# Eight buffers instead of four for the expert tiles' results and their addresses

## The chip, the cores and the metric

The kernel runs on 1 core of one Trainium2 chip. The metric is the device time of one execution in microseconds (us), the median of several runs. A profile of one further execution goes with it.

## The reference

Four stages work on x, 4 sequences of 512 tokens with 128 features. The second and the fourth are the same mixture of experts, with the same weights; the change lies in both.

```
x = x + attention(layernorm(x))
x = x + ffn(layernorm(x))        # list 0 of the kernel
x = x + scan_block(layernorm(x))
x = x + ffn(layernorm(x))        # list 1 of the kernel

# ffn, for each of the 2048 tokens:
scores = sigmoid(xf @ Wg.T + bg + bias)                  # 8 experts
top_scores, top_idx = top_k(scores, 2)
h  = gelu(einsum('td,ehd->teh', xf, W1) + b1)            # 128 -> 512
eo = einsum('teh,edh->ted', h, W2) + b2                  # 512 -> 128
combined = einsum('ted,te->td', eo, weights)             # the 2 chosen experts
shared   = gelu(xf @ Ws1.T + bs1) @ Ws2.T + bs2
```

## The kernel before

Each engine has its own stream of instructions, in an order written out by hand, and semaphores join them. In the ffn every token row is first scattered to `rows_dram` at a place sorted by expert, twice (once for each chosen expert). Then the sorted rows are worked off as a list of NT = 39 tiles of 128 rows, each of one expert. The results are scattered back to `y_dram` in token order, read again in four pieces and added to x with their weights (`combine`). The program has two such lists of 39 tiles, 78 tiles in all.

Every engine goes through a list in a loop over k. LAG is 3, so that in one turn of the loop different tiles are at different steps:

- SyncE (SP) loads the rows of tile s into `xg`, one of 7 buffers (L491). Load n waits until GpSimd has taken the addresses of tile n-7 (`goes_to_ready`) and TensorE has turned that tile.
- TensorE (PE): `turn(k)` transposes tile k (L1182, 2 matmuls), `up(k-1)` adds the bias (L1189, 4) and multiplies by W1 (L1194, 12), `down(k-3)` multiplies by W2 (L1205, 12).
- ScalarE (ACT): the gelu (L831) into `hid_t` and its high half (L836).
- VectorE (DVE), in this order in a turn of the loop: `turned(k)` copies the transposed tile to `xgT` (L1636), `low(k-2)` makes the low half of the hidden values (L1642), `results(k-3)` copies the result from PSUM to `y_t` (L1650).
- GpSimd (POOL): `address(k)` makes the rows of `y_dram` to which tile k goes, first `result_row` (L652), then `goes_to` (L654), and `store(k-3)` issues the indirect DMA from `y_t` to `y_dram` (L661), which reads its addresses from `goes_to`.

`y_t`, `result_row` and `goes_to` have YT buffers each. Two waits guard them, in `address` on GpSimd and in `results` on VectorE. Both ask that the scatter of tile n-YT has landed:

```
if n >= YT:
    pool.wait_ge(y_stored[n % YT], 16 * (n // YT))     # address(s), ahead of L652
...
if n >= YT:
    dve.wait_ge(y_stored[n % YT], 16 * (n // YT))      # results(s), ahead of L1650
```

The scatter of tile k-4 is issued in turn k-1 of GpSimd's loop, straight ahead of `address(k)`. After a list SyncE waits for every `y_stored` semaphore before it reads `y_dram` back (L497). `xgT`, `hid_t` and `y_t` are parts of one SBUF tensor, `arena`; the profile shows them, `yg` and the shared expert's `hid` under that name. The profile's `probs` is `hid16_t` in the lists, `qk_sb` is `xg`, and `heads_arena` holds other stages' tiles.

Of the kernel before, what the change touches and what calls it, by code (L numbers as in the profile page):

```python
# [10 lines left out]
F16 = mybir.dt.float16  # L11
# [3 lines left out]
P = 128  # L15
D = 128
# [9 lines left out]
F = 512  # L26
# [73 lines left out]
SPARE = P * NT + 2  # L100
RESULTS = SPARE + 2 * B * L
TILES_OF = B * L // P
XG, GT, HT, YT = 7, 3, 3, 4
LAG = 3
S_AT = TILES_OF
ROW_AT = S_AT + NT
# [71 lines left out]
def hybrid_block_kernel(nc, x_in, wqkv_in, wo_in, bo_in, w1_in, b1_in, w2_in, b2_in, wg_in, gate_rows_in,  # L178
# [3 lines left out]
    with ExitStack() as ctx:  # L182
        def sb(name, shape, dt=F32):
            return ctx.enter_context(nc.sbuf_tensor(name, shape, dt))
# [102 lines left out]
        arena = sb("arena", [P, 2 * X * F])  # L287
# [15 lines left out]
        def part(t, at, shape, dt=F32):  # L303
            size = int(np.prod(shape)) * (1 if dt == F32 else 2) // (1 if dt == F32 else 4)
            names = " ".join("abcd"[:len(shape)])
            sizes = dict(zip("abcd", shape))
            flat = t[:, at:at + size]
            return (flat if dt == F32 else flat.bitcast(dt)).rearrange(f"p ({names}) -> p {names}", **sizes)
# [10 lines left out]
        hid = part(arena, 0, [C, L])  # L319
        hid16 = part(arena, 2048, [2, C, L], F16)  # L320
        yg = part(arena, 4096, [2, TT, 2, D])
        xgT = part(arena, 6656, [GT, 2, P], F16)
        hid_t = part(arena, 7040, [HT, F])
        y_t = part(arena, 8576, [YT, D])
        xcv = part(probs_words, 0, [2, 2, L])
        hid16_t = part(probs_words, 2048, [HT, 2, F], F16)
        bias_tmp = heads_arena[:, 2048:3072]
# [1532 lines left out]
```

## Time and profile before

| | |
|---|---|
| median of 3 runs | 892.85 us (888.28 to 895.38) |
| profiled execution, its own time | 894.25 us |
| span of that execution | 892.4 us |
| TensorE / VectorE / ScalarE / GpSimd busy | 67% / 52% / 39% / 39% of the span |
| list 0, first to last scatter of results issued | 392.34 to 546.44 us |
| list 1, first to last scatter of results issued | 720.02 to 871.86 us |

Busy time is the share of the whole span. The profile's chain of waits goes back from the last instruction through what released each step, so its lines are time that the end of the program stood on. The times inside the profile belong to the one profiled execution, which took 894.25 us, 1.4 us more than the median.

### The profile page before, as it was taken

To read this page: it belongs to the slowest core of one execution; us is meant where nothing else is said; L and a number is where in the kernel's file an instruction comes from. 1 tells how busy PE (TensorE), PEld (TensorE's weight loads), DVE (VectorE), ACT (ScalarE), POOL (GpSimd) and SP (SyncE) were. 2 spreads that over 40 slices of the span, in tenths; PEclk is the share of its full clock that TensorE was granted. 3 is DMA by queue.
4 is the path that set the end of the run, shared out by engine and by line. 5 is a ranking of instruction groups with operands and counts; after the bars stand their busy time and mean duration, and the time that the engine had idled before them with its cause. 6 is when DMAs were issued, how large, how long until landed. Compare 5 with 4: busy or idle time off the path is not lost. (4 is left out here: it accounts for less than half of the span.)

```text
span 892.4 us, 16950 instructions
## 1 busy us (share of the span) xinstructions
PE 594.1 (67%) x5836; PEld 402.2 (45%) x5836; DVE 466.1 (52%) x1241; ACT 344.4 (39%) x462; POOL 349.9 (39%) x447
## 2 busy tenths in 40 slices
PE   2588888888885635578776750567676588676730
PEld 1454445444443413466655640234354376555520
DVE  5877776776772555533222221678867543222214
ACT  1355456556652424335332320225254354332310
POOL 4152080190001575534544453114335445444550
PEclk9699999999997757789877785667687799877875
DMA  8995000000000000111110102100000111111104
GB/s 297 328 334 161 2 1 1 1 2 1 1 2 27 24 7 28 38 45 38 31 31 25 37 19 77 35 0 25 7 19 24 35 46 32 31 30 31 35 18 150
DMA packets 45146, 46.37 MB, mean 52 GB/s; under 512 B 5369, under 2 KB 42386, under 8 KB 44810
## 3 DMA queue, kind: packets, MB, share of 16 engines
q1 hardware_dynamic: 40522, 35.91, 13.5%
q0 software_dynamic: 4544, 9.38, 3.1%
q8 instruction: 52, 0.85, 0.4%
q14 instruction: 28, 0.23, 0.1%
HBM read 16.75 MB, written 28.52 MB: 51 GB/s over the span
## 5 line engine op out<-in xcount | busy, mean ns | idle before, releaser
L1650 DVE COPY arena<-ps 128x128 f32<-128x128 f32 x78 | 22.7, 292 | 211.3 <-DMA y_dram<-arena,goes_to 177.4
L831 ACT ACTIVATE arena<-ps,up_back 128x512 f32<-128x512 f32 x78 | 53.6, 687 | 194.5 <-PE ps L1194 194.5
L1194 PE MATMUL ps<-arena,w 128*128 128x128 f16 x936 | 96.6, 246 | 45.3 <-DVE arena L1636 45.0
L1384 DVE TENSOR_REDUCE row_maxima<-ps 128x2 f32<-128x256 f32 (+3 forms) x128 | 99.0, 817 | 42.8 <-PE ps L958 42.5
L710 ACT ACTIVATE probs<-ps 128x768 f32<-128x768 f32 (+1 forms) x96 | 82.5, 884 | 81.2 <-PE ps L983 81.2
L512 POOL TENSOR_TENSOR rstd<-var_eps,minus_half 128x4 f32<-128x4 f32 x16 | 17.0, 1060 | 222.6 <-DVE var_eps L1321 222.6
L1205 PE MATMUL ps<-w,probs 128*128 x936 | 95.2, 248 | 10.8 <-DVE probs L1642 10.7
L1194 PEld LDWEIGHTS ps<-arena,w 128*128 x936 | 72.2, 106 | 65.9 <-issue 55.5
L661 POOL DMA_INDIRECT y_dram<-arena,goes_to x78 | 85.0, 1090 | 34.5 <-POOL goes_to L654 20.9
L643 POOL DMA_INDIRECT rows_dram<-probs,idx x64 | 69.0, 1078 | 52.8 <-DVE idx L1582 33.0
L1205 PEld LDWEIGHTS ps<-w,probs 128*128 128x128 f16 x936 | 77.0, 111 | 21.9 <-issue 12.3
L652 POOL TENSOR_SCALAR result_row<-qk_sb,list_end 128x1 f32<-128x1 f32 x78 | 29.4, 377 | 132.0 <-DMA y_dram<-arena,goes_to 120.9
L1003 PE MATMUL ps<-probs,v_tok 128*16 128x256 f32 (+3 forms) x512 | 74.7, 434 | 2.5 <-ACT probs L710 2.5
L1642 DVE SCALAR_TENSOR_TENSOR probs<-arena,hid_scale,probs 128x512 f16<-128x512 f32 x78 | 58.2, 746 | 4.5 <-ACT probs L836 4.5
L836 ACT ACTIVATE probs<-arena,hid_scale 128x512 f16<-128x512 f32 x78 | 56.3, 721 | 2.6
L1189 PE MATMUL ps<-which,bias_rows 128*128 128x128 bf16 x312 | 37.4, 254 | 20.4 <-issue 20.0
L654 POOL TENSOR_SCALAR goes_to<-result_row,grids 128x1 int32<-128x1 f32 x78 | 46.7, 599 | 7.3
L1003 PEld LDWEIGHTS ps<-probs,v_tok 128*16 128x16 f32 x512 | 24.2, 96 | 47.7 <-issue 35.4
L953 PE MATMUL ps<-heads_arena 48*128 48x128 bf16 (+3 forms) x256 | 37.6, 308 | 11.6 <-DVE row_maxima L1384 6.4
L978 PE MATMUL ps<-q2T,heads_arena 50*128 50x512 bf16 (+3 forms) x256 | 38.5, 310 | 9.0 <-ACT probs L710 7.2
L1189 PEld LDWEIGHTS ps<-which,bias_rows 128*128 128x128 bf16 x312 | 22.1, 112 | 32.2 <-issue 31.4
L1159 PE MATMUL ps<-w,arena 128*128 128x128 f16 x384 | 26.2, 230 | 13.3 <-DVE arena L1616 8.9
(234 smaller groups left out, 1111.7 us busy)
## 6 DMA issues: line engine op xcount, KB each, us to landing
rows_dram<-grids SPq DMA_DIRECT2D x2, 8840.0 KB, 44.1
qk_sb<-rows_dram SPq DMA_DIRECT2D x78, 65.0 KB, 1.8
arena<-in_w SPq DMA_DIRECT2D x2, 2304.0 KB
arena<-y_dram SPq DMA_DIRECT2D x8, 512.0 KB, 4.0
y_dram<-arena,goes_to POOLq DMA_INDIRECT x78, 2.4
x_all<-in_x SPq DMA_DIRECT2D x4, 256.0 KB, 8.1
rows_dram<-probs,idx POOLq DMA_INDIRECT x64
out_x<-x_all SPq DMA_DIRECT2D x4, 256.0 KB, 3.7
```

The costliest lines, as they stand in the source:

```text
L643: nc.gpsimd.indirect_dma_start(rows_dram[r].ap(), bass.IndirectOffsetOnAxis(ap=idx[:, r, b, t, k:k + 1], axis=0), xrow_words[:, b % 2, t, ...
L654: nc.gpsimd.tensor_scalar(goes_to[:, n % YT:n % YT + 1], result_row[:, n % YT:n % YT + 1], grids[:, SPARE_AT + s:SPARE_AT + s + 1], None, ...
L661: nc.gpsimd.indirect_dma_start(y_dram.ap(), bass.IndirectOffsetOnAxis(ap=goes_to[:, n % YT:n % YT + 1], axis=0), y_t[:, n % YT, :], None). ...
L710: nc.scalar.activation(probs[:, n % 2, :, PROB_AT[u]:PROB_AT[u] + size], ps[:, of:of + 2, 0:size], ACT.Exp).then_inc(slot_free[slot_of(("T ...
L831: nc.scalar.activation(hid_t[:, n % HT, :], ps[:, of, :], ACT.Gelu, scale=up_back[:]).then_inc(bank_free[of], 1)
L836: nc.scalar.activation(hid16_t[:, n % HT, 0, :], hid_t[:, n % HT, :], ACT.Identity, scale=hid_scale[:]).then_inc(high_t_ready, 1)
L1003: mm = pe.matmul(ps[quadrant:quadrant + VW, PV_BANK, j * P:L], v_tok[:, a % 2, j, 2 * p + h, :], probs[:, n % 2, h, at:at + size], start=( ...
L1189: pe.matmul(ps[:, to, c * P:(c + 1) * P], bias_rows[:, c * P:(c + 1) * P], which[:, s:s + 1].broadcast_to([P, P]), start=(c == 0), stop=Fa ...
L1194: mm = pe.matmul(ps[:, to, c * P:(c + 1) * P], w1[:, w, bass.ds(expert[s], 1), c * P:(c + 1) * P].rearrange("p o f -> p (o f)"), xgT[:, (r ...
L1205: mm = pe.matmul(ps[:, to, 0:D], hid16_t[:, n % HT, v, c * P:(c + 1) * P], w2[:, w, bass.ds(expert[s], 1), c, :].rearrange("p o d -> p (o ...
L1384: ins = nc.vector.tensor_reduce(row_maxima[:, t, 2 * p:2 * p + 2], ps[:, of:of + 2, o:o + keys], AX.X, ALU.max)
L1642: nc.vector.scalar_tensor_tensor(hid16_t[:, n % HT, 1, :], hid_t[:, n % HT, :], hid_scale[:], hid16_t[:, n % HT, 0, :], ALU.mult, ALU.subt ...
```

## The change

YT goes from 4 to 8. `y_t`, `result_row` and `goes_to` get 8 buffers, there are 8 `y_stored` semaphores, and the two waits above ask for tile n-8. To make room in the arena, `xgT`, `hid_t` and `y_t` start 512 words earlier, directly behind `yg` (which ends at word 6144); `y_t` ends at word 9088 as before. Neither an instruction nor the order on an engine changes; the waits do. SyncE waits for 8 semaphores in place of 4 after each list.

```diff
-XG, GT, HT, YT = 7, 3, 3, 4
+XG, GT, HT, YT = 7, 3, 3, 8
...
-        xgT = part(arena, 6656, [GT, 2, P], F16)
-        hid_t = part(arena, 7040, [HT, F])
-        y_t = part(arena, 8576, [YT, D])
+        xgT = part(arena, 6144, [GT, 2, P], F16)
+        hid_t = part(arena, 6528, [HT, F])
+        y_t = part(arena, 8064, [YT, D])
```

GpSimd's stream in list 0 before, from the first scatter on (L661, store(0)): each following L652 waits for the scatter that stands just ahead of it.

```order
138 L661 DMA y_dram<-arena,goes_to 9090x128 [waits bank_free1,goes_to_ready]
139 L652 TENSOR_SCALAR result_row<-qk_sb,list_end 128x1 [waits y_stored0,xg_loaded4]
140 L654 TENSOR_SCALAR goes_to<-result_row,grids 128x1 [waits pool_step]
141 L661 DMA y_dram<-arena,goes_to 9090x128 [waits bank_free4,goes_to_ready]
142 L652 TENSOR_SCALAR result_row<-qk_sb,list_end 128x1 [waits y_stored1,xg_loaded5]
```

The same place with the change: the four L652 of tiles 4 to 7 wait for their rows alone.

```order
138 L661 DMA y_dram<-arena,goes_to 9090x128 [waits bank_free1,goes_to_ready]
139 L652 TENSOR_SCALAR result_row<-qk_sb,list_end 128x1 [waits xg_loaded4]
140 L654 TENSOR_SCALAR goes_to<-result_row,grids 128x1 [waits pool_step]
141 L661 DMA y_dram<-arena,goes_to 9090x128 [waits bank_free4,goes_to_ready]
142 L652 TENSOR_SCALAR result_row<-qk_sb,list_end 128x1 [waits xg_loaded5]
```

The first `y_stored0` on GpSimd now stands at tile 8, whose wait is for the scatter of tile 0, issued five turns of the loop before. On VectorE the same is seen at L1650, here in the difference of the two streams for tiles 4 and 5:

```order
-L1650 COPY arena<-ps 128x128 [waits y_stored0,bank_full5]
 L1636 COPY arena<-ps 128x256 [waits bank_full1,bank_full6]
 L1642 SCALAR_TENSOR_TENSOR probs<-arena,hid_scale,probs 128x512 [waits high_t_ready]
-L1650 COPY arena<-ps 128x128 [waits y_stored1,bank_full0]
+L1650 COPY arena<-ps 128x128 [waits bank_full0]
```

Only the semaphore of the scatter has left the row; the bank that TensorE fills (`bank_full`) stays.

## Rows read from the trace of the kernel before

**Rows 1.** The page's chain that ended last, by line
```profile
DMA y_dram<-arena,goes_to 10%; POOL goes_to L654 2%; POOL result_row L652 1%; DMA arena<-y_dram 1%; DVE x_all L1665 1%; POOL rows_dram L643 1%; PE ps L1194 0%; DMA rows_dram<-probs,idx 0%; POOL y_dram L661 0%; DMA qk_sb<-rows_dram 0%; PE ps L1189 0%; POOLq L182 0%; SPq L490 0%; PE ps L1182 0%; PE ps L1205 0%
```

**Rows 2.** Who waited for whom in list 0: us in total, times, longest
```profile
DVE arena L1650 <- DMA y_dram<-arena,goes_to: 90.0, 28, 5.0
POOL result_row L652 <- DMA y_dram<-arena,goes_to: 62.5, 35, 3.5
...
POOL result_row L652 <- DMA qk_sb<-rows_dram: 5.4, 4, 4.4
```

**Rows 3.** The chain in order of time, one turn of list 1
```profile
767.41 2.50 DMA y_dram<-arena,goes_to
770.09 0.37 POOL result_row L652
770.56 0.76 POOL goes_to L654
771.59 2.45 DMA y_dram<-arena,goes_to
```

**Rows 4.** Timeline of GpSimd's scatters: tiles 0, 35, 36 of list 0; 0, 35, 38 of list 1
```profile
392.34 1.44 POOL L661 DMA_INDIRECT y_dram<-arena,goes_to  x1 [5.28 <-DVE arena L1650]
...
542.54 1.07 POOL L661 DMA_INDIRECT y_dram<-arena,goes_to  x1 [0.38 <-POOL goes_to L654]
543.91 0.96 POOL L661 DMA_INDIRECT y_dram<-arena,goes_to  x1 [0.30 <-issue]
...
720.02 1.44 POOL L661 DMA_INDIRECT y_dram<-arena,goes_to  x1 [4.57 <-DVE arena L1650]
...
867.96 1.07 POOL L661 DMA_INDIRECT y_dram<-arena,goes_to  x1 [0.38 <-POOL goes_to L654]
...
871.86 0.96 POOL L661 DMA_INDIRECT y_dram<-arena,goes_to  x1 [0.31 <-issue]
```

**Rows 5.** Timeline of TensorE in list 1: tile turns while VectorE did not hold it
```profile
719.37 0.40 PE L1189 MATMUL ps<-which,bias_rows 128*128 128x128 bf16 x4 [0.34 <-issue]
...
720.64 1.13 PE L1205 MATMUL ps<-w,probs 128*128 x12
...
760.35 0.40 PE L1189 MATMUL ps<-which,bias_rows 128*128 128x128 bf16 x4 [0.39 <-issue]
```

**Rows 6.** Busy time by stretch: PE, PEld, DVE, ACT, POOL, then PEclk, DMA, GB/s
```profile
100.00:120.00 20.00, 17.09 (x182) 10.37 (x178) 12.10 (x27) 9.94 (x14) 5.84 (x10) 0.91 0.01 2
...
712.00:718.00 6.00, 5.70 (x53) 5.43 (x54) 1.55 (x5) 2.82 (x4) 1.99 (x6) 0.50 0.24 60
718.00:761.00 43.00, 36.83 (x447) 29.27 (x446) 17.20 (x43) 21.13 (x30) 20.72 (x30) 1.00 0.13 37
761.00:860.00 99.00, 67.70 (x661) 53.78 (x660) 25.95 (x68) 30.99 (x44) 49.47 (x70) 0.78 0.10 30
```

**Rows 7.** Timeline in list 1: an address that stood free, and one beside VectorE's L1642
```profile
735.87 0.29 POOL L654 TENSOR_SCALAR goes_to<-result_row,grids 128x1 int32<-128x1 f32 x1
...
770.41 0.74 DVE L1642 SCALAR_TENSOR_TENSOR probs<-arena,hid_scale,probs 128x512 f16<-128x512 f32 x1
770.56 0.75 POOL L654 TENSOR_SCALAR goes_to<-result_row,grids 128x1 int32<-128x1 f32 x1
```

**Rows 8.** All addresses and scatters: ns min/median/max, then first and last start; landing
```profile
L654 POOL TENSOR_SCALAR goes_to<-result_row,grids x78: 292/755/802, 383.5 to 867.3; 128x1 int32<-128x1 f32 x78
L661 POOL DMA_INDIRECT y_dram<-arena,goes_to x78: 954/1067/1591, 392.3 to 871.9; - x78
...
DMA to landing us min/median/max: 2.2/2.4/4.4
```

**Rows 9.** Timeline of TensorE at the half clock in list 1: L1189 of two turns, L1205
```profile
714.56 0.63 PE L1189 MATMUL ps<-which,bias_rows 128*128 128x128 bf16 x4
...
716.48 0.63 PE L1189 MATMUL ps<-which,bias_rows 128*128 128x128 bf16 x4
...
767.73 1.49 PE L1205 MATMUL ps<-w,probs 128*128 x12
```

## Prediction

> **What bounds the kernel now.** I read the chain of waits first. Its largest entry is the landing of the result scatters, 10% of the span [rows 1]. The chain follows the end of the program back, and these landings are those of list 1. The wait table of list 0 shows the same picture there: VectorE waits 90.0 us ahead of L1650 and GpSimd 62.5 us ahead of L652, both for the scatter `y_dram<-arena,goes_to` [rows 2].
>
> The chain in order of time shows the loop that closes [rows 3]. A scatter issued at 767.41 lands after 2.50 us; GpSimd's `result_row` starts at 770.09; `goes_to` at 770.56; the next scatter at 771.59. That is 2.50 + 0.18 + 0.47 + 1.03 = 4.18 us for one tile. Nothing else is in it. The reason is in the code: turn k issues store(k-4) at the end of turn k-1, and address(k) then asks at once for that same scatter to have landed, since tile k takes over the buffer of tile k-4. So only one scatter is ever on its way, although there are four buffers. VectorE's `results(k)` waits for the same landing, and since VectorE works in order, the copy of the next transposed tile stands behind it, and TensorE behind that.
>
> The scatters give the length of it [rows 4]. List 0: tile 0 at 392.34, tile 35 at 542.54, 35 turns in 150.20 us, 4.29 us each. List 1: 720.02 to 867.96, 147.94 us, 4.23 us each. Some turns are longer than 4.18 because a landing takes 2.2 to 4.4 us [rows 8].
>
> **How fast the other engines are without it.** The trace shows this, because TensorE runs ahead at the start of each list until all buffers between it and the scatters are full. In list 1 its L1189 starts at 719.37 and, 14 turns later, at 760.35 [rows 5]: 2.93 us a turn. TensorE bounds this stretch itself: it is busy 36.83 of 43 us at a granted clock of 1.00 [rows 6], and what it idles is the 0.39 us of "issue" ahead of L1189. VectorE and ScalarE are busy for 17.20 and 21.13 of those 43 us. From 761 on, with the buffers full, TensorE is busy for 68% of the time and the clock falls to 0.78.
>
> **The change, part by part.**
>
> The wait on GpSimd. With eight buffers address(k) asks for the scatter of tile k-8, issued at the end of turn k-5: four more turns lie between, 11.7 us at 2.93 us each, against a longest landing of 4.4 us. The wait goes altogether.
>
> What GpSimd itself then needs for a tile: from `result_row` to `goes_to` 0.47 us [rows 3]; from `goes_to` to the scatter 1.03 us when `goes_to` takes 0.76 us [rows 3]; from a scatter to what follows it 1.37 us, of which 1.07 is the issue itself (542.54 to 543.91) [rows 4]. The sum is 2.87 us. With the short `goes_to` of 0.29 us [rows 7] and 0.38 us behind it (ahead of the scatter at 542.54) [rows 4] it is 2.51 us. GpSimd is therefore just quicker than TensorE's 2.93 us, and it is next in line.
>
> The wait on VectorE. `results(k)` now asks for tile k-8; GpSimd may lag by several tiles before it is felt. What is late next there is TensorE's L1205, that is TensorE itself.
>
> SyncE's loads of rows. Load n waits for address(n-7). Addresses will come every 2.93 us, and a load has seven turns of lead. In list 0 GpSimd waited for rows four times, 5.4 us in total, nearly all at the list's start [rows 2]. I cost this at nothing; its cover is those seven turns.
>
> The moved buffers. `xgT`, `hid_t` and `y_t` keep their sizes and partitions and shift by 512 words. They touch `yg`, but do not overlap it, and no instruction changes its shape: 0. The trace has no row on the placement within a partition. SyncE's four more waits per list stand ahead of L497 and are satisfied except for the last scatters: under 0.1 us each, 0.2 us in all.
>
> The sum, for one list. From the scatter of tile 0 to that of tile 35: 35 x 2.93 = 102.6 us. Saved: 150.2 - 102.6 = 47.6 us in list 0 and 147.9 - 102.6 = 45.3 us in list 1. The last three scatters took 3.9 us (867.96 to 871.86 [rows 4]), since their tiles had long been computed. Now TensorE still has to work out tiles 36 to 38: one turn without a transposition (some 2.7 us), one L1205 (1.1 us), and the last one behind ScalarE and VectorE (another 1.3 us), 5.1 us. That gives back 1.2 us in each list. Together 92.9 - 2.4 = 90.5 us.
>
> I give back 3 us more. Clock: even dense work has dips. The stretch from 100 to 120 us shows 0.91 with TensorE as busy as in the lists' free part [rows 6]. At the half clock turn and up take 1.92 us together (714.56 to 716.48) and L1205 1.49 us [rows 9], 3.4 us a tile, 0.5 us more than 2.93. With a twentieth of the 70 turns there it costs 2 us. GpSimd: the first scatter of each list took 1.44 us and the longest 1.59 against a median of 1.07 [rows 4, 8]; with so little room below 2.93 I take 1 us for those.
>
> So: 894.25 (the profiled execution) - 90.5 + 3 + 0.2 = 807 us. That execution lies 1.4 us above the median, which makes 805.5; I forecast **806 us**.
>
> **A row that speaks against this.** When `goes_to` runs beside VectorE's L1642 it takes 0.75 us, when it stands free 0.29 us [rows 7]; the median of all 78 is 0.755 [rows 8]. In the blocked part that meeting is forced, because one landing releases both engines. L1642 reads two tensors from SBUF and takes 0.74 us. The Trainium skill says in "SBUF — State Buffer", section "SBUF: two separate sides", that VectorE and GpSimd share one pair of SBUF ports under an exclusive lock, held for a whole instruction, also when the VectorE instruction has two SBUF inputs; the loser blocks fully. The trace agrees with it for `goes_to`. By the row the price is 0.47 us, already in my 2.87. Taken at its worst, the rule would let one L1642 per tile block GpSimd for its whole 0.74 us on top of the short loop of 2.51: 3.25 us a tile, which is rival 1.
>
> **The rivals.**
>
> 1. GpSimd becomes the bound. For: its loop is 2.87 us against 2.93, a scatter's issue can take 1.59, and at the new pace VectorE's 0.74 us may fall on `result_row`, `goes_to` or the issue in turn. Against: one VectorE instruction blocks one of them, and GpSimd was rarely hit while it ran out of step with VectorE (`goes_to` 0.29 at 735.87 [rows 7]). Price: 3.25 us a tile is 70 x 0.32 = 22 us, 828 us. If every scatter's issue took 1.59 with the long `goes_to`, it would be 3.39 a tile and 70 x 0.46 = 32 us, 838 us.
>
> 2. The clock does not stay up. For: before, the lists' later part ran at 0.78, and list 1 starts at 0.50 [rows 6]. Against: it fell there only with TensorE idle a third of the time, and was 1.00 for the whole 43 us of free running, which is what the rest would now look like. Price: if a clock of 0.78 stayed, 44% of the time would be at half clock: 70 x 0.44 x 0.5 = 15 us, 821 us. All at half clock: 70 x 0.5 = 35 us, 841 us.
>
> 3. The landing is not what holds the loop, and another wait takes its place at the same length: SyncE's loads also hang on the addresses, so rows could arrive just as late. Then the time stays near 893 us. Against: of 39 tiles of list 0 only four `result_row` waited for rows [rows 2], and TensorE ran 14 turns at 2.93 us while addresses came every 4.2 us.
>
> 4. Slower than before: a scatter's issue on GpSimd becomes dear once an earlier one is still on its way, which the loop never allowed so far. The place is L661 in the middle of a list. A tile then costs 1.50 + issue + 0.30 us on GpSimd, so it decides from an issue of 2.4 us on; at 3 us a tile takes 4.8 us and 70 x 0.55 = 39 us are lost, 933 us. Against: at each list's end four scatters are issued 1.30 us apart, each before the last can have landed (2.2 us at the least [rows 8]), with 0.96 us of issue [rows 4].
>
> **How the numbers follow.** TensorE's pace in both lists, 798 to 813 us: 0.63. Rival 1, 813 to 838: 0.20. Rival 2, 811 to 841: 0.10. Rival 3, or a gain under 1%: 0.03. Rival 4: 0.02. A better time than 798 us would need a turn under 2.85 us: 0.02. The range 797 to 832 us takes in the first case, most of the next two, and leaves out their dear ends. A measurement of this kernel tells about 1% (9 us) from no change: faster by over 1% 0.95, within 1% 0.03, slower 0.02.
>
> **What the profile of the changed kernel would show.** Right: the landing of `y_dram<-arena,goes_to` gone from the chain and the wait tables, TensorE's lines and "issue" in its place; L1189 every 2.93 us up to tile 38; PEclk near 1.00 from 6 us after each list's start; first to last scatter 108 us in each list; addresses and scatters about one tile behind VectorE. Rival 1: GpSimd without idle time, VectorE's L1650 again waiting for landings in the second half of a list, L661 or L654 longer. Rival 2: PEclk below 0.9 with L1189 at 3.2 us or more. Rival 3: `result_row` waiting for `qk_sb<-rows_dram`. Rival 4: L661 over 2 us. What would make me wrong most easily is the small gap of 0.06 us between the paces of GpSimd and TensorE.

## The result and the profile after

The changed kernel takes 800.42 us (median of 4 runs, 799.66 to 800.60) against 892.77 us. The ratio is 0.8975, with a 95% interval of 0.8953 to 0.8997: 10% faster. Its profiled execution took 800.33 us, with a span of 798.5.

First the page's chain of waits of the changed kernel, by engine and by line, which answers to [rows 1]:

```profile
PE 12%; issue 2%; DMA 2%; POOL 1%; DVE 1%; SPq 0%; POOLq 0%; DVEq 0%
PE ps L1205 5%; PE ps L1194 5%; PE ps L1189 2%; DMA arena<-y_dram 1%; DVE x_all L1665 1%; POOL rows_dram L643 1%; PE ps L1182 1%; POOL y_dram L661 0%; DMA rows_dram<-probs,idx 0%; DMA y_dram<-arena,goes_to 0%; DMA qk_sb<-rows_dram 0%; SPq L490 0%; SPq L491 0%; POOLq L182 0%; DVE arena L1650 0%
```

The landing of the scatters has gone from 10% to 0%, and TensorE's three lines of a tile stand in its place. The wait table of list 0 (us in total, times, longest), against [rows 2]:

```profile
DVE arena L1650 <- PE ps L1205: 63.4, 37, 1.8
ACT arena L831 <- PE ps L1194: 53.8, 37, 1.6
POOL y_dram L661 <- DVE arena L1650: 38.6, 35, 4.0
...
PE ps L1189 <- issue: 15.0, 36, 0.6
```

No engine waits for a scatter any more. GpSimd waits for VectorE, VectorE and ScalarE wait for TensorE, and TensorE, but for 0.4 us once, waits only for its own "issue", which is idle time that no event of the profile explains. The scatters in the timeline of GpSimd, list 0 (tiles 0, 35, 38) and list 1 (the same), as in [rows 4]:

```profile
387.32 1.29 POOL L661 DMA_INDIRECT y_dram<-arena,goes_to  x1 [4.01 <-DVE arena L1650]
...
489.88 1.11 POOL L661 DMA_INDIRECT y_dram<-arena,goes_to  x1 [0.99 <-DVE arena L1650]
...
495.30 0.95 POOL L661 DMA_INDIRECT y_dram<-arena,goes_to  x1 [0.30 <-issue]
...
669.17 1.07 POOL L661 DMA_INDIRECT y_dram<-arena,goes_to  x1 [4.52 <-DVE arena L1650]
...
771.77 1.08 POOL L661 DMA_INDIRECT y_dram<-arena,goes_to  x1 [1.05 <-DVE arena L1650]
...
777.07 0.96 POOL L661 DMA_INDIRECT y_dram<-arena,goes_to  x1 [0.31 <-issue]
```

From tile 0 to tile 35 both lists take 102.6 us, 2.93 us a turn, where they took 150.2 and 147.9. From tile 0 to tile 38 they take 108.0 and 107.9 us in place of 154.1 and 151.8: 46.1 and 43.9 us less, 90.0 together. The spans differ by 93.9 us. The rest is that list 0's first scatter came 5.0 us earlier (387.32 against 392.34), less 0.3 us lost between the lists (173.9 against 173.6) and 0.9 us lost behind the last scatter (21.4 against 20.5).

The busy time of the two lists (PE, PEld, DVE, ACT, POOL, then PEclk, DMA share, GB/s), against [rows 6]:

```profile
386.00:490.00 104.00, 88.84 (x1064) 70.45 (x1063) 43.04 (x108) 50.16 (x72) 61.93 (x106) 1.00 0.16 44
668.00:772.00 104.00, 89.08 (x1065) 70.43 (x1063) 42.92 (x107) 49.82 (x71) 63.15 (x106) 1.00 0.16 44
```

TensorE is busy 85% of the time in both, and its clock stands at 1.00 from the first scatter to tile 35. The addresses and scatters of both lists (ns min/median/max, then landing), against [rows 8]:

```profile
L654 POOL TENSOR_SCALAR goes_to<-result_row,grids x78: 292/292/618, 378.4 to 770.4; 128x1 int32<-128x1 f32 x78
L661 POOL DMA_INDIRECT y_dram<-arena,goes_to x78: 954/1087/1453, 387.3 to 777.1; - x78
...
DMA to landing us min/median/max: 2.2/2.4/4.5
```

The scatters are as slow as before, 2.4 us in the median and 4.5 at the longest; only no engine waits for them inside a list. With a turn of 2.93 us and a landing of 2.4 us there is even now mostly one scatter on its way at a time: what the change buys is not several at once, but other work done during the landing. The median `goes_to` has fallen from 755 to 292 ns.

### The profile page after: what moved, and what is told of

Same layout as the page of the kernel before. It is cut to its first block and busy times, and to the rows that moved or that the text cites. A ratio compares the mean times of both kernels' runs of the same rounds, so it can differ in the third digit from the quotient of the medians.

```text
span 798.5 us, 16946 instructions
## 1 busy us (share of the span) xinstructions
PE 566.2 (71%) x5836; PEld 377.7 (47%) x5836; DVE 466.9 (58%) x1241; ACT 344.6 (43%) x462; POOL 327.8 (41%) x447
## 5 line engine op out<-in xcount | busy, mean ns | idle before, releaser
L1384 DVE TENSOR_REDUCE row_maxima<-ps 128x2 f32<-128x256 f32 (+3 forms) x128 | 99.0, 817 | 44.1 <-PE ps L958 43.9
L661 POOL DMA_INDIRECT y_dram<-arena,goes_to x78 | 85.4, 1095 | 82.1 <-DVE arena L1650 73.9
L1650 DVE COPY arena<-ps 128x128 f32<-128x128 f32 x78 | 22.8, 292 | 127.4 <-PE ps L1205 127.3
L1194 PE MATMUL ps<-arena,w 128*128 128x128 f16 x936 | 87.0, 227 | 0.2
L1205 PE MATMUL ps<-w,probs 128*128 x936 | 85.2, 217 | 1.2 <-DVE probs L1642 0.8
L1205 PEld LDWEIGHTS ps<-w,probs 128*128 128x128 f16 x936 | 66.5, 96 | 15.9 <-issue 2.7
L1194 PEld LDWEIGHTS ps<-arena,w 128*128 x936 | 65.8, 99 | 12.0 <-issue 1.1
L1642 DVE SCALAR_TENSOR_TENSOR probs<-arena,hid_scale,probs 128x512 f16<-128x512 f32 x78 | 58.8, 753 | 4.2 <-ACT probs L836 3.8
L1189 PE MATMUL ps<-which,bias_rows 128*128 128x128 bf16 x312 | 32.3, 227 | 30.7 <-issue 30.7
L953 PE MATMUL ps<-heads_arena 48*128 48x128 bf16 (+3 forms) x256 | 37.8, 310 | 11.6 <-DVE row_maxima L1384 6.3
L1189 PEld LDWEIGHTS ps<-which,bias_rows 128*128 128x128 bf16 x312 | 18.7, 100 | 43.5 <-issue 43.5
L652 POOL TENSOR_SCALAR result_row<-qk_sb,list_end 128x1 f32<-128x1 f32 x78 | 30.4, 390 | 16.4 <-DMA qk_sb<-rows_dram 6.6
L958 PE MATMUL ps<-mask_qk,neg_eye 64*128 64x128 bf16 x512 | 35.1, 222 | 0.0
```

The source lines that it names most:

```text
L661: nc.gpsimd.indirect_dma_start(y_dram.ap(), bass.IndirectOffsetOnAxis(ap=goes_to[:, n % YT:n % YT + 1], axis=0), y_t[:, n % YT, :], None). ...
L1189: pe.matmul(ps[:, to, c * P:(c + 1) * P], bias_rows[:, c * P:(c + 1) * P], which[:, s:s + 1].broadcast_to([P, P]), start=(c == 0), stop=Fa ...
L1194: mm = pe.matmul(ps[:, to, c * P:(c + 1) * P], w1[:, w, bass.ds(expert[s], 1), c * P:(c + 1) * P].rearrange("p o f -> p (o f)"), xgT[:, (r ...
L1205: mm = pe.matmul(ps[:, to, 0:D], hid16_t[:, n % HT, v, c * P:(c + 1) * P], w2[:, w, bass.ds(expert[s], 1), c, :].rearrange("p o d -> p (o ...
L1384: ins = nc.vector.tensor_reduce(row_maxima[:, t, 2 * p:2 * p + 2], ps[:, of:of + 2, o:o + keys], AX.X, ALU.max)
L1642: nc.vector.scalar_tensor_tensor(hid16_t[:, n % HT, 1, :], hid_t[:, n % HT, :], hid_scale[:], hid16_t[:, n % HT, 0, :], ALU.mult, ALU.subt ...
```

## The experiments

The theory: the loop was closed by the wait in `address(k)` on GpSimd, for the scatter that stood directly ahead of it. VectorE's wait, the larger of the two for the scatter, follows from it. The rivals: the place in the arena, VectorE's wait, or the number of buffers as such. Three runs take the change apart, a fourth reaches the same without a buffer more.

**Only the place in the arena.** Four buffers, the three offsets of the change.

```diff
-        xgT = part(arena, 6656, [GT, 2, P], F16)
-        hid_t = part(arena, 7040, [HT, F])
-        y_t = part(arena, 8576, [YT, D])
+        xgT = part(arena, 6144, [GT, 2, P], F16)
+        hid_t = part(arena, 6528, [HT, F])
+        y_t = part(arena, 8064, [YT, D])
```

> Four buffers everywhere, as before; only xgT, hid_t and y_t stand 512 words earlier in the arena, as in the changed kernel. If the gain is all a matter of the waits: 893 us, within 0.5% of before, and a scatter every 4.2 to 4.3 us in both lists. If the place in the arena had a part in it: below 888 us.

Measured: 893.62 us against 893.47, ratio 1.0006 (0.9982 to 1.0030). The place is worth nothing that this could measure. List 0's first scatter came at 388.55 us in this profile, 3.8 us earlier than in that of the kernel before, with the same waits; in the next run, with the arena at its old place, it came at 388.59. So most of the 5.0 us ahead of list 0 is a difference between executions, not an effect of the change. The scatters came every 4.37 us in list 0 (388.55 to 541.58 for 35 turns) and every 4.25 in list 1; the first is a little over what was expected.

**Eight addresses, four results.**

```diff
+AT_N = 8
...
-        result_row = sb("result_row", [P, YT])
-        goes_to = sb("goes_to", [P, YT], I32)
+        result_row = sb("result_row", [P, AT_N])
+        goes_to = sb("goes_to", [P, AT_N], I32)
...
-                    if n >= YT:
-                        pool.wait_ge(y_stored[n % YT], 16 * (n // YT))
+                    if n >= AT_N:
+                        pool.wait_ge(y_stored[(n - AT_N) % YT], 16 * ((n - AT_N) // YT + 1))
...
```

> Eight buffers for the addresses (result_row, goes_to) alone; y_t keeps four, at its old place. Theory A (the wait in address() closes the loop; VectorE's wait for the same landing is only its echo): about 800 us, a scatter every 2.93 us. Theory B (VectorE's wait ahead of L1650, the largest in the wait table, is the one that counts): about 893 us. If each carries half of it: 845 us.

Measured: 800.73 us, ratio 0.8966 (0.8935 to 0.8996), with a turn every 2.93 us (388.59 to 491.13 for 35). The small address tiles carry the whole gain; `y_t` needs no more room, and four `y_stored` semaphores are enough.

**Four addresses, eight results.** The same split with AT_N = 4 and YT = 8 on the changed kernel.

> The other half: eight buffers of results y_t, addresses keep four. Theory A: 893 us, GpSimd still waits for each landing ahead of L652, 4.2 us a tile; TensorE only runs further ahead, some 18 tiles instead of 14, and then waits as before. Theory B: about 800 us.

Measured: 891.47 us, ratio 0.9980 (0.9953 to 1.0007). In list 1 tiles 0 to 35 took 146.7 us, 4.19 us each. The wait table of list 0 up to 500 us, in this kernel's line numbers (one more than in the kernel before), shows who waits now:

```profile
DVE arena L1651 <- PE ps L1206: 58.8, 31, 2.6
POOL result_row L653 <- DMA y_dram<-arena,goes_to: 48.1, 25, 3.5
...
PE ps L1183 <- DMA qk_sb<-rows_dram: 21.5, 16, 4.8
```

VectorE no longer waits for a scatter at all, and it doesn't help. GpSimd still does. TensorE, which I had expected to run further ahead and then wait as before, now waits for rows, because SyncE may load tile n only when address(n-7) is made. So with four addresses the landing reaches TensorE by a second way, through the rows.

**Four buffers, the scatter ahead of the address.**

```diff
                 for k in range(NT + LAG):
+                    if k >= LAG:
+                        store(k - LAG)
                     if k < NT:
                         address(k)
-                    if k >= LAG:
-                        store(k - LAG)
```

> Four buffers of everything; on GpSimd the turn of the loop is written in the other order, store(k-3) ahead of address(k). Address(k) still waits for the scatter of tile k-4, but that one now stands a whole turn back. Theory A in its sharp form (what costs is that a scatter and the wait for its landing stand next to each other in GpSimd's stream, not the number of buffers): 800 to 806 us, a scatter every 2.93 us. If eight buffers of slack are needed for the landings that take up to 4.4 us: 810 to 840 us. If the number of buffers itself counts: 893 us.

Measured: 800.91 us, ratio 0.8972 (0.8941 to 0.9003), with a turn every 2.93 us (387.59 to 490.16 for 35). The theory holds in its sharp form: one turn between a scatter and the wait for its landing is enough, and two lines in the other order give it. Late landings are still waited for, but cost nothing: ahead of L652 GpSimd waits for one 9 times in both lists, 4.5 us in all and 0.9 at most. (The table puts a further 44.0 us ahead of L661 down to landings. In the code L661 waits for VectorE's copy and not for a landing, and the changed kernel has VectorE's L1650 in that place, so I read them as that wait.)

**Five buffers**, everything else as in the change (`YT` = 5).

> Five buffers in place of eight (y_t, result_row, goes_to and the semaphores), arena as in the changed kernel. Address(k) asks for scatter k-5, which has one turn of 2.93 us between its issue and the wait: more than the usual landing of 2.4 us, less than the longest of 4.5. If one turn is enough, since a late landing only delays GpSimd, which has slack: 800 to 803 us. If all eight are needed: 810 us or more.

Measured: 806.05 us on a chip on which the kernel before takes 901.50, ratio 0.8940 (0.8895 to 0.8984). The absolute time missed what was expected by 3 us, on a chip that is slower with the kernel before too; the ratio is that of eight buffers. Tiles 0 to 35 of list 1 took 102.6 us (675.12 to 777.72). The longest landings cost nothing at five either: GpSimd waits ahead of L652 for a landing 8 times, 4.1 us in all.

**How much room GpSimd has.** One further small instruction per tile, which brings nothing but its time; in the second run three (`range(3)`).

```diff
+                    for _ in range(1):
+                        link(nc.gpsimd.tensor_scalar(spare_row[:], xg_words[:, n % XG, D:D + 1], list_end[:, s:s + 1],
+                                                     xg_words[:, n % XG, D + 1:D + 2], ALU.is_lt, ALU.add))
                     nc.gpsimd.tensor_scalar(goes_to[:, n % YT:n % YT + 1], result_row[:, n % YT:n % YT + 1],
```

> The changed kernel with one more GpSimd instruction per tile, a copy of L652's operation into a spare column (about 0.47 us with its link). It tells how much room GpSimd has. By the prediction's loop of 2.87 us there are 0.06 us of room: 3.34 us a tile, 70 x 0.41 = 29 us more, 829 us. By the changed trace's short goes_to (0.29 us) the loop is 2.5 us: 2.98 us a tile, 800 to 806 us.

> As the run before with three such instructions per tile (1.4 us). GpSimd must now be the bound: 2.51 + 1.41 = 3.92 us a tile, 70 x 0.99 = 69 us more, 870 us; by the loop of 2.87 us it would be 4.28 a tile and 895 us.

Measured: one more: 809.05 us, ratio 0.8968 (0.8922 to 0.9013), 2.97 us a turn in list 0 (395.29 to 499.23) and 2.98 in list 1. Three more: 880.69 us, ratio 0.9766 (0.9718 to 0.9814), 3.99 and 4.04 us a turn. With one more instruction GpSimd's stream is full (69 of 78 scatters wait for GpSimd's own `goes_to`), at the 2.51 + 0.47 = 2.98 us that were expected, but it doesn't lengthen the list: from first to last scatter it takes 108.1 and 108.5 us, where the changed kernel takes 108.0 and 107.9. TensorE keeps its pace, and the eight buffers take up the 1 to 2 us by which GpSimd falls behind. The 3 us over the five buffers' time on the same chip stand mostly ahead of list 0, whose first scatter came at 395.29 us against 392.88. With three more, GpSimd is the bound of the whole, 0.1 us a turn over the 3.92 expected.

So GpSimd's room in the changed kernel is some 0.4 us a tile, not the 0.06 of the prediction; what I feared as rival 1 needs at least that much more per tile to show. That 2.51 us fits so well is partly luck. It has 1.37 us for the step from a scatter to what follows it, which is the distance of two scatters at a list's end; from a scatter to `result_row` the changed kernel takes 1.11 to 1.17 us, and a turn of GpSimd in which nothing holds it took 2.28 us (700.58 to 702.86, shown further down). What the 2.51 us leave out is VectorE's L1642. In the changed kernel `result_row` took 0.83 us at 703.99, beside L1642 from 703.82 on, and 0.90 us at 706.71, against 0.38 when it stands free; with one more instruction the mean `result_row` and `goes_to` of list 0 are 0.47 and 0.46 us.

**TensorE's gap ahead of L1189.** Its register load of the expert's number (in `up`, straight ahead of L1189), moved out of `up` into `pick(s)`, called ahead of `turn(k)`; then, in another run, four loads together ahead of every fourth `up`.

```diff
+                    if 1 <= k <= NT:
+                        pick(k - 1)
                     if k < NT:
                         turn(k)
```

> The changed kernel with TensorE's register load of the tile's expert number moved ahead of turn(k), so that it runs under the matmuls of the turn before. If the 0.39 us of issue ahead of L1189 is this load's delay, a turn falls from 2.93 to 2.54 us, which is where GpSimd's loop of 2.5 us stands: 70 x 0.39 = 27 us less, 773 us, or some us more if GpSimd and VectorE get in each other's way (by a GpSimd loop of 2.87 us: 796 us). If the gap has another cause, or only moves ahead of L1182: 800 us.

```diff
                 def up(s):
-                    expert[s] = pe.value_load(tile_expert[0:1, s:s + 1], min_val=0, max_val=E)
+                    if s % 4 == 0:
+                        for i in range(s, min(s + 4, NT)):
+                            pick(i)
```

> The changed kernel with TensorE's register loads of four tiles' expert numbers together, ahead of every fourth up(). Moving a single load had only moved the gap. If the gap is a wait that the first load pays and the three behind it share (the pipeline has to run empty, or the read has to come back): 2.93 - 0.3 = 2.63 us a tile, 20 us less than the changed kernel. If each load costs its 0.39 us by itself: no difference, four gaps in one, 0 to 3 us.

Measured: the first 804.05 us on the slower chip, ratio 0.8921 (0.8877 to 0.8966), 2.91 to 2.92 us a turn; the second 802.65 us, ratio 0.8967 (0.8951 to 0.8983). The first is 2 us under the five buffers' 806.05 beside it (the changed kernel itself was not run on that chip), the second 2 us over the changed kernel's 800.59 beside it; the 27 and 20 us hoped for are not there. In the first the gap goes along with the load and now stands ahead of L1182, 0.56 and 0.50 us long at 422.08 and 424.95. In the second the timeline of TensorE shows four loads at once:

```profile
422.14 0.27 PE L1182 MATMUL ps<-ident_f,qk_sb 128*128 128x128 f16 x2
...
424.32 0.27 PE L1182 MATMUL ps<-ident_f,qk_sb 128*128 128x128 f16 x2
427.07 0.40 PE L1194 MATMUL ps<-which,bias_rows 128*128 128x128 bf16 x4 [2.47 <-issue]
```

Four loads leave TensorE without work for 2.47 us, 0.62 each, which is more than four single gaps of 0.39. So the loads share nothing. The turn without a load takes 2.18 us (422.14 to 424.32), and the two before it 1.90 and 1.95 (from 418.29 and 420.19). All are shorter than 2.93 by more than the gap of 0.39 us. The matmuls themselves come quicker there: the twelve of L1199, the W1 product in this kernel's lines, take 0.66 us up to the start of the next group (418.86 to 419.52), where the changed kernel takes 1.02 (422.20 to 423.22), with the granted clock at 1.00 in both places. So TensorE's 2.93 us, 85% of it busy by the profile, is not the fastest that TensorE goes through these matmuls.

Over four turns nothing is won: from one gap's end to the next it is 11.6 to 11.7 us (392.14 to 403.75, 415.33 to 427.07), as four turns of 2.93 are. The granted clock was 0.83 from 390 to 420 us and 0.73 from 450 to 480 in this kernel, where it is 1.00 in the changed one, so slow turns stand beside the quick ones. Whether the lower clock takes back what the quick turns gain, or something else sets the same pace, such as the rate at which instructions reach TensorE, no run tells apart.

**The changed kernel again**, on the same chip as that last run and the next.

> The changed kernel itself once more, as the measure for the two beside it on the same chip: ratio to before 0.893 to 0.900, 2.93 us a tile.

Measured: 800.59 us, ratio 0.8957 (0.8942 to 0.8972).

**Two products in place of three** in the lists' `up` and `down`: the low half of the weights is left out, 8 of the 30 matmuls of a tile.

```diff
+TWO = [(0, 0), (0, 1)]
...
-                        for w, v in PRODUCTS:
+                        for w, v in TWO:
```

> The changed kernel with two of the three products in up() and down() of the lists: the low half of the weights is left out, 8 of the 30 matmuls of a tile. TensorE then needs 2.93 - 8 x 0.09 = 2.2 us a tile. If TensorE is the bound of the changed kernel, the time falls until GpSimd's loop of 2.51 us holds it: 70 x 0.42 = 29 us less than the changed kernel; by a GpSimd loop of 2.87 us only 4 us less. If TensorE isn't the bound: no change.

Measured: 765.91 us against 893.78 us, ratio 0.8573 (0.8555 to 0.8590), 34.7 us less than the changed kernel beside it, where 29 were expected. Tiles 0 to 35 took 85.5 us in list 0 (2.44 us each, 386.91 to 472.38) and 87.3 us in list 1 (2.50). The wait rows of the view of `goes_to` (what GpSimd's idle time ahead of its scatter ended with, us and times) show who holds it:

```profile
  POOL goes_to L655: 25.9, 69
  DVE arena L1651: 6.9, 2
```

In the changed kernel 66 of 78 scatters waited for VectorE's L1650 (73.9 us); here two do. So TensorE with its stream of instructions was the bound of the changed kernel, whatever sets its pace, and GpSimd's loop of 2.44 to 2.50 us is what comes next.

## Why the prediction was right

The forecast was 806 us, and its main case, at 0.63, was that TensorE's pace sets both lists. It came out at 800.4, by that mechanism.

- The loop: shown. With four addresses the turn is 4.2 us even when VectorE's wait is gone; with eight addresses alone, or with four and one turn between scatter and wait, it is 2.93 us.
- VectorE's wait as an echo: shown by the same pair of runs. It was the largest wait for a scatter in its table (ScalarE's for TensorE, 98.0 us, was larger still) and worth nothing by itself.
- TensorE's 2.93 us, read from the 14 free turns at the start of list 1 [rows 5]: measured 2.93 over 35 turns in both lists.
- The tail, 5.1 us forecast for the last three scatters: 5.4 and 5.3 us (489.88 to 495.30, 771.77 to 777.07).
- The moved buffers, costed at 0: ratio 1.0006.
- The sum for the lists, 90.5 us: 90.0 us.
- The 3 us that I gave back: 2 us for the clock, which never fell (1.00 in both lists), and 1 us for long issues on GpSimd, which cost nothing. These 3 us and the 5.0 us ahead of list 0 make 8.0; 1.7 us go the other way (0.5 in the lists, 0.3 between them, 0.9 behind them). That leaves 6.3 of the 6.6 us between 807, the forecast for the profiled execution, and its 800.33. The 5.0 us were mostly chance and no part of the mechanism.
- GpSimd's loop of 2.87 us was the weak step. Its 1.37 us from a scatter to what follows it measured 1.11 to 1.17 ahead of `result_row`. It also took the long `goes_to` of 0.76 us [rows 3], which came of both engines being released by one landing. Released in turn, GpSimd makes its address while VectorE does not run L1642 (`result_row` and `goes_to` from 420.77 to 421.53 us, L1642 from 421.94 on), and the median fell to 0.29 us. The rule of the Trainium skill in "SBUF — State Buffer", section "SBUF: two separate sides", that one engine of the pair blocks the other, is seen in the trace now and then, as 0.62 us for the longest `goes_to` and 0.90 for the longest `result_row`, but not at each turn; rival 1 built on it at its worst gave 828 us.
- Rival 4, a dearer issue of a scatter while another is on its way, was hardly put to the test: at 2.93 us a turn that is the case only behind a late landing and at a list's end. There the last scatter's issue took 0.95 and 0.96 us, as before (0.96 [rows 4]).

One stretch of list 1 shows that TensorE does not notice a late GpSimd. The timeline of GpSimd's scatters:

```profile
695.66 1.07 POOL L661 DMA_INDIRECT y_dram<-arena,goes_to  x1 [1.18 <-DVE arena L1650]
700.58 1.05 POOL L661 DMA_INDIRECT y_dram<-arena,goes_to  x1 [3.04 <-issue]
702.86 1.07 POOL L661 DMA_INDIRECT y_dram<-arena,goes_to  x1 [0.39 <-POOL goes_to L654]
705.58 1.07 POOL L661 DMA_INDIRECT y_dram<-arena,goes_to  x1 [0.38 <-POOL goes_to L654]
708.37 1.07 POOL L661 DMA_INDIRECT y_dram<-arena,goes_to  x1 [0.38 <-POOL goes_to L654]
```

One scatter came 2 us late, after 3.04 us in which GpSimd waited for nothing that the profile shows. The next ones follow after 2.28, 2.72 and 2.79 us until the lag is made up. TensorE's L1189 went on meanwhile, at 698.06, 700.94 and 703.89 us.

## What to carry to other kernels

Count buffers in the order of one engine's stream: what matters is how much work stands between the issue of a transfer and the first wait for it, not how many buffers there are. Four buffers with the wait directly behind the transfer left a turn at 4.2 us; the same four with the two steps in the other order were worth as much as eight. When several engines wait for one landing, ask which of them closes the loop: here the wait with the smaller entry did. How fast the loop would be once the wait was gone could here be read at its start, before the buffers were full.

## What the runs showed of the hardware that was not expected

- A load of a register on TensorE's sequencer leaves TensorE idle for 0.39 us ahead of L1189 and for 0.50 to 0.56 ahead of L1182, and for 0.6 us each when four stand together, although matmuls are issued straight ahead of it.
- At the same granted clock of 1.00 twelve matmuls took 1.02 us in the changed kernel and 0.66 in turns without a load. The cause was not tested.
- The runs of the kernel before spread over 1% on one chip (889.01 to 898.11 us in 19 runs), those of the changed kernel over 0.15% (800.55 to 801.65 and 799.66 to 800.60, 4 runs each). On one and the same chip it was 0.4% in 7 runs against 0.14% in 4 (891.39 to 894.86, 800.55 to 801.65). The landings of 2.2 to 4.5 us were in the loop and are no longer; that this is the cause was not tested, and the run with two products spreads over 0.5% without them in its loop.
- Chips differ: on one of them the kernel before took 901.50 us, 0.9% more than on the others (892.77 to 893.78).
